# Turning the routed tokens without TensorE, and ordering accumulating writes by expert

## What is computed

```
x = x + _L0_xattn_ref(_layernorm(x), ctx, ...)   # 16 heads, 2048 keys, 8-bit q/k/v/probabilities
x = x + _L0_ffn_ref(_layernorm(x), ...)
...
scores = jnp.sqrt(jax.nn.softplus(logits))       # logits = flat @ router_w.T, E = 32
_, idx = jax.lax.top_k(scores + expert_bias, K)  # K = 4
topv = topv / (topv.sum(axis=-1, keepdims=True) + 1e-20)
g = jnp.clip(x @ wg.T, -7, 7); u = jnp.clip(x @ wu.T, -7, 7)   # I = 256
silu(g) * u @ wd.T                               # per expert, times the token's share, summed
out = sum over experts + the same with the shared weights
```

## Time and profile before

| | us |
|---|---|
| median of 3 runs | 1444.52 (1441.58 to 1453.22) |
| profiled execution | 1447.9 |
| its span | 1446.2 |
| TensorE busy | 1276.8 (88%) |
| VectorE busy | 976.3 (68%) |
| GpSimd busy | 874.8 (60%) |
| ScalarE busy | 800.0 (55%) |
| granted clock, mean | 0.978 |

### The profile page before, as it was taken

How to read it: one execution, slowest core, us unless ns; L and a number is a source line. 1 busy time by engine, 2 the same in 40 slices (tenths; PEclk the granted TensorE clock), 3 DMA queues, 4 the chain that set the end, 5 groups by cost and what they waited for, 6 DMA issues and landing times.

```text
span 1446.2 us, 28685 instructions
## 1 busy us (share of the span) xinstructions
PE 1276.8 (88%) x7890; PEld 634.9 (44%) x7891; DVE 976.3 (68%) x1886; ACT 800.0 (55%) x1030; POOL 874.8 (60%) x894
## 2 busy tenths in 40 slices
PE   8999578888888888888887879999999999999995
PEld 3444134444444444444443434444444444444442
DVE  4567799999999999999999646823333333333332
ACT  2224499999999999999999742221222222222221
POOL 3223388899899999899888812243444444444443
PEclk9999799999999999999999889999999999999998
DMA  7565977786677667666677866465677777686442
GB/s 249 131 153 118 174 122 138 142 146 145 133 145 145 139 132 142 142 144 137 144 139 132 183 204 168 93 170 119 151 194 212 200 197 179 142 221 140 91 75 31
DMA packets 398568, 215.53 MB, mean 149 GB/s; under 512 B 356903, under 2 KB 357031, under 8 KB 398514
## 3 DMA queue, kind: packets, MB, share of 16 engines
q1 hardware_dynamic: 378338, 176.05, 51.7%
q0 software_dynamic: 20176, 38.83, 15.0%
HBM read 100.28 MB, written 37.49 MB: 95 GB/s over the span
## 4 chain that ended last, share of the span: by engine, by line
PE 36%; DVE 20%; issue 19%; DMA 13%; POOL 4%; ACT 4%; SPq 1%; DVEq 1%; POOLq 0%; ACTq 0%
PE psS L815 15%; DMA out_y<-mem 9%; DVE mem L579 7%; DVE mem L595 7%; PE psS L823 6%; PE psS L450 3%; POOL mem L669 3%; DMA mem<-mem 3%; ACT mem L536 2%; PE psS L1671 2%; PE psT L1280 1%; PE psP L807 1%; PE psAV L421 1%; DVE mem L1078 1%; PE psAV L1658 1%
## 5 line engine op out<-in xcount | busy, mean ns | idle before, releaser
L536 ACT ACTIVATE mem<-mem 128x2048 uint8<-128x2048 f32 x256 | 534.3, 2088 | 46.0 <-POOL mem L652 42.2
L669 POOL TENSOR_SCALAR mem<-mem 128x2048 bf16<-128x2048 uint8 x256 | 486.0, 1899 | 26.8 <-DMA mem<-mem 6.4
L450 PE MATMUL psS<-mem 128*128 128x512 bf16 x1024 | 313.2, 388 | 112.3 <-DVE mem L579 54.2
L815 PE MATMUL psS<-mem 128*128 (+1 forms) x752 | 348.6, 605 | 0.0
L595 DVE TENSOR_SCALAR_CACHE_REDUCE mem<-psS,mem 128x1024 f32<-128x1024 f32 x256 | 327.5, 1279 | 3.0 <-PE psS L450 2.9
L579 DVE TENSOR_SCALAR_CACHE_REDUCE mem<-psS 128x1024 f32<-128x1024 f32 x256 | 312.4, 1220 | 14.0 <-PE psS L450 11.8
L849 DVE TENSOR_SCALAR mem<-psS 128x512 f32<-128x512 f32 x94 | 64.9, 691 | 321.7 <-PE psS L815 312.5
L843 ACT ACTIVATE mem<-mem 128x256 f32<-128x256 f32 x94 | 39.1, 416 | 352.9 <-DVE mem L849 349.4
L1212 POOL DMA_INDIRECT out_y<-mem x78 | 124.3, 1593 | 170.4 <-DMA out_y<-mem 150.2
L815 PEld LDWEIGHTS psS<-mem 128*128 128x128 f32 x752 | 136.3, 191 | 146.7 <-issue 143.5
L823 PE MATMUL psS<-mem 128*128 (+1 forms) x376 | 179.0, 598 | 2.0 <-ACT mem L837 2.0
(11 more groups left out here) (210 smaller groups left out, 1177.1 us busy)
## 6 DMA issues: line engine op xcount, KB each, us to landing
mem<-in_moe_w SPq DMA_DIRECT2D x64, 768.0 KB, 5.7
mem<-xn_dram SPq DMA_DIRECT2D x32, 256.0 KB, 3.0
xn_dram<-mem SPq DMA_DIRECT2D x29, 256.0 KB, 2.2
mem<-in_x SPq DMA_DIRECT2D x28, 256.0 KB, 2.9
mem<-mem SPq DMA_TRANSPOSE x292, 3.1
mem<-in_ctx_in SPq DMA_DIRECT2D x16, 256.0 KB, 3.4
out_y<-mem SPq DMA_DIRECT2D x16, 256.0 KB, 2.2
mem<-in_wkv SPq DMA_DIRECT2D x2, 1024.0 KB, 7.8
```

The lines of the kernel that those rows point to most:

```text
L450: last = nc.tensor.matmul(psS[c][:, k * D:(k + 1) * D], qT[pm][:, hm, :], kT[:, hm, c * HALF + k * D:c * HALF + (k + 1) * D], start=True, ...
L536: nc.scalar.activation(p8[slot], S[slot], ACT.Exp, bias=NB[:, slot:slot + 1], scale=sq[p][:, h:h + 1], accum_out=Z[p][:, h:h + 1]).then_in ...
L669: nc.gpsimd.tensor_scalar(pb[slot], pT[slot].bitcast(U8).rearrange("p (j q b) -> p j b q", b=2, q=P), 1.0, 0.0, ALU.mult, ALU.add).then_in ...
L815: last = nc.tensor.matmul(bankG[o], xT[o if xo is None else xo][:, c, :], w(c * 2 * I, 2 * I), start=(c == 0), stop=(c == DC - 1))
```

## The change

1. In the routed loop the first three tiles are still transposed by TensorE. Later ones are turned by DVE in 32x32 blocks (`dve_turn`, four instructions of 64 partitions x 256 for a tile, three tiles ahead of use). That leaves half of the blocks of each 64x64 square in the wrong quarter of the partitions. ACT places them (`act_place`): one copy of the whole tile, then four copies of 32 partitions over the blocks that lie wrong. The buffers lie where the shared expert's weights were.
2. The hidden transposes of k - 1 move into the middle of the up projection of k (`pe_up_around`).
3. Token shares are copied in the DVE step three tiles ahead (`dve_keep`), into one of four columns; gathers are issued when that copy is done, for a tile seven ahead of the POOL step, from row numbers of their own (`next_rows`).
4. Accumulating writes count on two semaphores by parity. A write waits for the one two before, and for the one just before only where the tile's expert differs from the last one's: `after_changes` holds 16 there and 0 elsewhere, POOL loads it into a register and adds it to the count that it waits for.
5. SP issues the four value pieces behind the four key pieces.

```diff
+        changes = cut(NT)
+        after_changes = cut(NT, I32)
...
-        rows_by = rows_sb.rearrange("p (g l) -> p g l", l=MU)
-        tile_rows = [cut(2, I32) for _ in range(MU)]
-        kept = [cut(1) for _ in range(2)]
+        tile_rows = [cut(1, I32) for _ in range(MU)]
+        next_rows = [cut(1, I32) for _ in range(MU)]
+        kept_all = cut(MU)
+        kept = [kept_all[:, l:l + 1] for l in range(MU)]
+        share_last = cut(1)
+        turned_at = shared_w
+        blocks = [turned_at[:, i * D:(i + 1) * D].rearrange("p (c t b) -> p c t b", c=DC, t=4) for i in range(2)]
+        xT_routed = [turned_at[:, (2 + i) * D:(3 + i) * D].rearrange("p (c t) -> p c t", c=DC) for i in range(MU)]
+        assert (2 + MU) * D <= EW
...
-            v_.tensor_scalar(te_sb, bankX[:, E + P:E + P + NT], E - 1.0, None, ALU.min).then_inc(te_ready, 1)
+            then(v_.tensor_scalar(te_sb, bankX[:, E + P:E + P + NT], E - 1.0, None, ALU.min))
+            then(v_.memset(changes[:, 0:1], 0.0))
+            then(v_.tensor_tensor(changes[:, 1:NT], te_sb[:, 1:NT], te_sb[:, 0:NT - 1], ALU.not_equal))
+            v_.tensor_scalar(after_changes, changes, 16.0, None, ALU.mult).then_inc(te_ready, 1)
...
         def pool_gather_next(pool, kk, l):
             k = MU * kk + l
-            pool.wait_ge(tile_rows_ready, k - SHARED + 1)
-            apart(pool, k)
             pool.wait_ge(share_kept, k - SHARED + 1)
             apart(pool, k)
-            pool_gather(pool, l, tile_rows[l][:, 1:2])
+            if isinstance(kk, int):
+                if k - SHARED < BY_PE:
+                    pool.wait_ge(tokens_tr, k + 1)
+                pool_gather(pool, l, rows_sb[:, k - SHARED + MU:k - SHARED + MU + 1])
+            else:
+                pool.wait_ge(next_rows_ready, k - SHARED - 2 * MU + 2)
+                apart(pool, k)
+                pool_gather(pool, l, next_rows[l])
+
+        def turns(kk, l):
+            return 2 * (kk - FIRST) + l // 2
 
         def pool_step_routed(pool, kk, l):
             k = MU * kk + l
             if not later(kk, l):
-                pool_gather_next(pool, kk, l)
-            pool_gather_next(pool, kk + (l + 1) // MU, (l + 1) % MU)
+                pool.wait_ge(te_ready, 1)
+            changed = pool.value_load(column(after_changes[0:1, :], k - SHARED), min_val=0, max_val=16)
+            if isinstance(kk, int) and l < BY_PE - 1:
+                for n in ((0, 1), (2,))[l]:
+                    pool_gather_next(pool, kk, n)
+            pool_gather_next(pool, kk + (l + BY_PE) // MU, (l + BY_PE) % MU)
             pool.wait_ge(y_ready, k + 1)
             apart(pool, k)
-            if later(kk, l):
-                pool.wait_ge(added, 16 * (k - SHARED))
+            own = l % 2
+            pool.wait_ge(tile_rows_ready, k - SHARED + 1)
+            apart(pool, k)
+            if due(turns(kk, l)):
+                pool.wait_ge(added[own], 16 * turns(kk, l))
                 apart(pool, k)
-            pool_add(pool, tile_rows[l][:, 0:1], y[l], added)
+            if isinstance(kk, int) and l in (1, 2):
+                pool.wait_ge(added[1 - own], 16)
+            elif later(kk, l):
+                pool.wait_ge(added[1 - own], changed + 16 * (turns(kk, l) + own - 1))
+                pool.sem_inc(passed, 1)
+            pool_add(pool, tile_rows[l], y[l], added[own])
...
+        def pe_up_around(pe, k, w, stationary, between):
+            pe.wait_ge(xT_ready, k + 1)
+            pe.wait_ge(gu_ready, k - 1)
+            o = between[1]
+            for c in range(DC):
+                if c == DC // 2 and between[0]:
+                    pe_hidden(pe, k - 1, 1 - o)
+                last = nc.tensor.matmul(bankG[o], stationary[:, c, :], w(c * 2 * I, 2 * I), start=(c == 0), stop=(c == DC - 1))
+            last.then_inc(gu_mm, 1)
+
         def pe_routed(pe, kk, l):
             k, o, b = MU * kk + l, l % 2, (l - 1) % 2
+            by_pe = isinstance(kk, int) and l < BY_PE
...
-            pe_gathered(pe, kk + (l + 1) // MU, (l + 1) % MU)
-            if later(kk, l):
-                pe_hidden(pe, k - 1, b)
+            if isinstance(kk, int) and l + 1 < BY_PE:
+                pe_gathered(pe, kk, l + 1)
             pe.wait_ge(expert_there, e + 1)
-            pe_up(pe, k, o, weights_of(e))
+            pe_up_around(pe, k, weights_of(e), xT[o] if by_pe else xT_routed[l], (later(kk, l), o))
...
+        def act_place(act, kk, l, pieces):
+            k, i = MU * kk + l, l % 2
+            whole = xT_routed[l].rearrange("p c (t b) -> p c t b", t=4)
+            for piece in pieces:
+                if piece == 0:
+                    act.wait_ge(turned, k - SHARED - BY_PE + 1)
+                    if isinstance(kk, int) and k - SHARED < BY_PE + MU:
+                        act.wait_ge(down_mm, SHARED)
+                    else:
+                        act.wait_ge(gu_mm, k - MU + 1)
+                    nc.scalar.activation(xT_routed[l].rearrange("p c t -> p (c t)"),
+                                         blocks[i].rearrange("p c t b -> p (c t b)"), ACT.Copy).then_inc(placed, 1)
+                else:
+                    g, j = (piece - 1) // 2, (piece - 1) % 2
+                    to, of = slice(32 * (2 * g + j), 32 * (2 * g + j + 1)), slice(32 * (2 * g + 1 - j), 32 * (2 * g + 2 - j))
+                    if piece == 1:
+                        act.wait_ge(placed, 4 * (k - SHARED - BY_PE) + 1)
+                    last = piece == 4
+                    nc.scalar.activation(whole[to, :, 1 - j::2, :], blocks[i][of, :, j::2, :],
+                                         ACT.Copy).then_inc(xT_ready if last else placed, 1)
+
         def act_routed(act, kk, l):
             k, o, b = MU * kk + l, l % 2, (l - 1) % 2
+            n = (kk + (l + 2) // MU, (l + 2) % MU)
             if not later(kk, l):
                 act_tokens(act, k, o)
-            act_tokens(act, k + 1, b)
+            if isinstance(kk, int) and l + 1 < BY_PE:
+                act_tokens(act, k + 1, b)
             if later(kk, l):
                 act_hidden(act, k - 1, b)
+            if later(kk, l):
+                act_place(act, n[0], n[1], (0, 1))
             act_silu(act, k, o)
+            if later(kk, l):
+                act_place(act, n[0], n[1], (2, 3, 4))
...
-                dve.wait_ge(added, 16 * (k - SHARED - 2))
+            if not isinstance(kk, int):
+                dve.wait_ge(added[o], 16 * (turns(kk, l) - (l != MU - 1)))
             elif l < 2:
                 dve.wait_ge(y_stored[o], 16 * SHARED // 2)
-            nc.vector.tensor_scalar(y[l] if to is None else to, bankY[o], kept[o], None, ALU.mult).then_inc(y_ready, 1)
+            nc.vector.tensor_scalar(y[l], bankY[o], kept[l], None, ALU.mult).then_inc(y_ready, 1)
...
+        def dve_turn(dve, kk, l, h):
+            k, i = MU * kk + l, l % 2
+            if h == 0:
+                dve.wait_ge(tokens_in[l], 16 * (kk - FIRST + 1))
+                if isinstance(kk, int) and k - SHARED < BY_PE + 2:
+                    dve.wait_ge(down_mm, SHARED)
+                else:
+                    dve.wait_ge(xT_ready, k - 1)
+            rows_in = slice(64 * h, 64 * h + 64)
+            for g in range(2):
+                last = nc.vector.transpose(
+                    blocks[i][64 * g:64 * g + 64, :, 2 * h:2 * h + 2, :].rearrange("p c t b -> p c (t b)"),
+                    xg[l][rows_in, 0:D].rearrange("p (c g d) -> p c g d", c=DC, g=2)[:, :, g, :])
+            if h == 1:
+                last.then_inc(turned, 1)
+
+        def dve_keep(dve, kk, l):
+            k = MU * kk + l
+            e = expert_of(dve, k)
+            dve.wait_ge(tokens_in[l], 16 * (kk - FIRST + 1))
+            if not isinstance(kk, int) or kk > FIRST:
+                dve.wait_ge(y_ready, k - MU + 1)
+            nc.vector.tensor_copy(kept[l], xg[l][:, bass.ds(e + D, 1)]).then_inc(share_kept, 1)
+
+        def dve_next_rows(dve, kk, l):
+            k = MU * kk + l
+            nc.vector.tensor_copy(next_rows[l], column(rows_sb, k - SHARED + MU)).then_inc(next_rows_ready, 1)
 
         def dve_routed(dve, kk, l):
             k, o, b = MU * kk + l, l % 2, (l - 1) % 2
+            n = (kk + (l + BY_PE) // MU, (l + BY_PE) % MU)
             if not later(kk, l):
                 dve.wait_ge(te_ready, 1)
+                for first in range(BY_PE):
+                    dve_keep(dve, kk, first)
             dve_gate(dve, k, o)
-            e = expert_of(dve, k)
-            dve.wait_ge(tokens_tr, k + 1)
-            if later(kk, l - 1):
-                dve.wait_ge(y_ready, k - 1)
-            nc.vector.tensor_copy(kept[o], xg[l][:, bass.ds(e + D, 1)]).then_inc(share_kept, 1)
-            dve_tile_rows(dve, kk, l)
+            dve_turn(dve, n[0], n[1], 0)
             dve_hid(dve, k, o)
             if later(kk, l):
                 dve.wait_ge(share_kept, k - SHARED)
-                dve_routed_out(dve, k - 1, (l - 1) % MU)
```

(62 more changed lines are left out.)

10 lines of the change are left out of this document (2 added, 8 removed).

## The result

| | us |
|---|---|
| before, median of 4 runs | 1445.49 (1441.58 to 1453.22) |
| changed, median of 4 runs | 1390.89 (1388.49 to 1394.71) |
| ratio | 0.9618, 95% interval 0.9572 to 0.9664 |
| changed, profiled execution and its span | 1390.22, 1388.2 |

The side was right, the size was not, and one term of the sum had the wrong sign.

A forecast was written before the change was run, and what follows sets the result against it. TensorE was taken to bound the routed stage. -33.4 + 7.7 - 4 - 1.3 - 1.3 - 2.0 = -34.3 on the profiled 1447.9 gave 1413.6, or 1410 us for a median; range 1399 to 1431.

The forecast's parts named there:

- Part 1, the transposes: Routed loop, TensorE: token transposes leave its list, 76 x 0.44 = 33.4 us gone.
- Part 1, the second change of kind: Hidden transposes mid-up add a second matmul-transpose change: 0.10 us a tile (bounds 0 and 0.2), 7.7 us back.
- part 6: Attention loads on SP: value issues go behind the key pieces, scores start sooner; -2.0 us, bounds 0 and -4.8.
- Part 2, DVE: Routed tiles: four DVE transposes of 0.43 us each, DVE at 4.7 of about 5.6 us; cost 0, cover 1.0.
- Part 3, ACT: Routed tiles: ACT's added copies bring it to 3.1 of 5.6 us; cost 0, cover 0.5 us.
- Part 4, the writes: POOL's routed writes: fewer waits for predecessors and earlier gathers gain 4 of 7 us of stalls, bounds 0 and 7.
- the seam's 1.3: Second routed tile: TensorE's 1.32 us wait at 961.97 goes, hidden being behind half an up; -1.3 us.
- the rival in which it binds: Routed writes in flight together land no sooner: 5.83 us a tile instead of 5.66, +13, 1423 us; chance 0.12.
- the next rival: Nearly nothing gained in routed tiles: DVE transposes of 0.75, or writes at the full 6.06; 1430 to 1441 us; chance 0.08.
- Part 5: Ends of the routed stage: -1.3 us from an early TensorE wait, -1.3 from a gather ahead of the last write.

The follow-up runs named there:

- x3: The changed kernel, with TensorE also transposing four 128x128 identity pieces, read by nobody, at the head of each loop step; median 1424.85 us, ratio 0.9845.
- x1: The kernel before, with only the hidden transposes moved into the middle of the routed up projection; median 1433.66 us, ratio 0.9905.
- x7: The changed kernel with each DVE transpose done twice, once into a spare buffer that nobody reads; median 1402.58 us, ratio 0.9701.
- x2: The changed kernel with the hidden transposes back ahead of the whole up projection; median 1442.18 us, ratio 0.9971.
- x4: The changed kernel with after_changes 16 everywhere, so each accumulating write waits for the one before; median 1442.66 us, ratio 0.996.
- x8: The changed kernel with the edits of x3 and x4 together: identity transposes on TensorE and all writes serial; median 1434.32 us, ratio 0.9916.
- x6: The kernel before, with the value pieces issued behind the key pieces and nothing else; median 1443.46 us, ratio 0.9983.
- x5: The changed kernel with two value pieces issued between the key pieces again; median 1393.75 us, ratio 0.964.

## Why the prediction was wrong in size

**Part 1, the transposes: right.** 33.4 booked; x3 gives 34.0 for 74 tiles.

**Part 1, the second change of kind: this step failed.** "The up takes 3.54 where twice the down's 1.72 is 3.44: one boundary costs 0.10 ... I take 0.10, 7.7 us back." I predicted a tile of 5.63 us (5.97 - 0.44 + 0.10); it is 5.37. The 0.26 between them, times 77, is 20 us: 0.10 charged for a second boundary that costs nothing, and 0.15 of waiting, still in my tile, that the same edit removes. x1 shows that neither the second boundary nor the first costs anything, and that hidden falls to 0.22. The first 0.10 and the 0.05 in hidden were a wait too short to be listed as one: in 74 of 77 tiles hidden started within 0.3 us of the end of DVE's product, and the weight load behind it lost its head start. I had named that wait in the shared tile and given it no price in the routed ones. The sign of the term was wrong: the tile fell by 0.15 in x1, 11.6 us over 77 tiles, where I had +0.10 and +7.7. The medians' -11.5 agrees, though some of it is listed waits (1.3 at the seam) booked elsewhere, and the profiled loop gave 7.6, with 5.8 more of waits for gathered rows in it.

Stage by stage, between the spans: I had booked 2.0 us ahead of the first routed up, 31.0 in the loop and 1.3 behind it; 7.1, 52.4 and -1.5 came. So the loop holds 21.4 of the 23.7 us that the sum missed by. The start gave 5.1 more than booked, 3.4 of it ahead of anything that part 6 moves, and the end 2.8 less: that these two cancel in part is luck.

**Part 2, DVE: right at no cost,** with 0.44 for 0.43 a transpose. The cover was larger than I said: the product is ready 1.3 us before TensorE asks for it, where I had 1.0, and the fixed part of DVE's step is 2.0 us (x7), not 2.9 (my own terms add up to 2.98). x2 shows what it would have been without the move of part 1: 0.7 us a tile.

**Part 3, ACT: right.** 57 of 100 us busy, where 3.1 of 5.6 was said.

**Part 4, the writes: the gain in the old stalls about right, its weight badly underrated.** Over 76 distances the tile's mean was 6.06 for 5.97 before and is 5.40 for 5.37 now, so about 5 us of stalls went, 4 plus the seam's 1.3 booked. But I had measured the chain at 6.15 us a tile in the earlier trace rows and still priced the rival in which it binds at 5.83, "halfway"; only the next rival had "the full 6.06", and 1430 to 1441 with it. With every write serial, x4 measures 6.1 a write and 1442.7, not 1423. The rival's own condition, that writes in flight together land no sooner, did not come true: a write lands 4.9 us after its start at the median in the changed kernel as in x4, and two overlap. The two edits don't add: with serial writes the kernel without the token transposes (x4) is no faster than the one with them (x8), so that their 33 us exist only because the writes were relaxed. POOL's wait for landings fell from 150.2 to 76.0, not under half of 141 as I had said it should.

**Part 5: the seam's 1.3 came, the end is wrong in sign.** The last 24.6 us are 1.5 longer, where I had -1.3. The tail's waits of TensorE and POOL in the changed kernel:

```profile
1372.60 0.43 PE L819 MATMUL psP<-ident,mem 128*128 128x128 f32 x2 [3.42 <-issue]
```

```profile
1374.63 1.05 POOL L1224 DMA_INDIRECT mem<-xn_dram,mem  x1 [0.30 <-issue]
1379.57 1.59 POOL L1229 DMA_INDIRECT out_y<-mem  x1 [3.90 <-issue]
```

The gather is out of the last write's way, but that write still starts 1.3 us behind the last scaling's end at 1378.24: four semaphore waits stand ahead of it in POOL's queue, and none was tried alone. And the last hidden transposes wait 3.42 us for no engine (1.83 before). x1, whose only edit is the move of hidden, shows 3.88 there, and x2, which takes it back, 1.68. Over all profiles it is 1.7 to 2.0 with hidden first (before, x2, x6) and 3.4 to 3.9 with hidden mid-up (the other nine). So the move costs some 1.5 us or more at the end. Why is open: that TensorE's queue, held longer at the last hidden of the loop, starts later on the remaining loop checks, fits, and was not tested.

**Part 6: right** within its bounds: 1.6 us by position; 2.5 to 2.9 by medians, the changed kernel's interval and x5's overlapping.

**The parts in order,** by medians: hidden mid-up alone -11.5 (x1); from there to x3, the relaxed writes, the gathers further ahead, values behind keys, with TensorE still transposing, -8.8; the transposes off TensorE -34.0. Sum -54.3 of -54.6.

## What to carry to other kernels

Don't read a price for a change of instruction kind out of one start-to-start distance: subtract the bare instructions (here 12 x 0.43 + 0.44 + 0.22 = 5.82), and treat what is left, even 0.1 us, as a wait until another place in the trace shows it without a producer arriving just then. Here three tiles of the trace before had the answer. When two chains run at nearly the same pace, price a saving on one by the other's pace: with a serial chain of landings at some 6 us a tile, taking TensorE from 5.98 to 5.82 gave 11.5 us (x1), going on to 5.37 gave nothing more (x4), and with the chain relaxed it gave 34 (x3). Work on idle engines is free only where the chain through them has slack, so move the consumer before adding to the producer.

## What the runs showed of the hardware

- Fp32 transposes on DVE, 64 partitions x 256, take 0.437 us, as much as a plain operation of that length on 128 partitions; the Trainium skill's 311 ns ("VectorE: DVE Perf Modes", section "The three transpose paths") is for a 128x128 bf16 tile, which no run here has.
- POOL's write instructions kept their 1.59 us (1.587 to 1.614 over 78) beside DVE at 70 of 100 us, nearly half of it transposes. The lock of "SBUF — State Buffer" in the Trainium skill, weighed in part 4, does not show in them. Whether DVE's transposes can hold the shared port at all was not tested.
- The routed accumulating indirect writes of 128 rows land 4.9 us after they start at the median, 3.6 to 8.7 in x4 and 3.7 to 8.1 in the changed kernel. Two in flight do overlap: there three start at 1107.44, 1110.71 and 1113.96 and land at 1112.28, 1115.74 and 1119.87.
- A change between matmul and transpose on TensorE costs nothing that these traces show: with four of them a tile takes 5.82 us, 12 matmuls of 0.43, four transposes of 0.11 and two of 0.11.
- Stalls of TensorE cost more than their length. In x4, where it waits 2.3 us at 1096 and 5.3 at 1125, the granted clock is 0.90 over this stretch, so the lower level is granted in part of it (the row below); behind the wait before 1048.88 half an up takes 3.28 us in the records, not 1.88.

```profile
1090.00:1140.00 50.00, 42.34 (x100) 18.66 (x99) 28.02 (x76) 21.80 (x50) 19.59 (x15) 0.90 0.65 166
```
